# A decoder on one core: the clamp of the mixer's decay differences is computed on ScalarE instead of VectorE

## What is computed

```
dt = clip(softplus(dt + dt_bias), 0, 100)
A_cum = cumsum(dt * A)                                  # over the 128 tokens, falling, since A < 0
L = exp(where(l >= s, A_cum[l] - A_cum[s], -inf))       # the decays
Y = einsum('bzlhn,bzshn,bhzls,bzshp->bzlhp', C, B, L, hs * dt) + hs * D
out = rmsnorm_per_group(Y * silu(gate)) * norm_w @ out_proj_w.T
```

## Time and profile before

| | |
|---|---|
| time, median of 3 runs | 2916.17 us (2915.06 to 2918.78) |
| the profiled execution, its span from the first to the last instruction | 2919.1 us |
| PE busy | 2603.7 us (89%) |
| DVE busy | 1872.9 us (64%) |
| ACT busy | 1371.7 us (47%) |
| POOL busy | 1129.4 us (39%) |
| mixer stage | 382 to 1836 us of the span, 1454 us |

### The profile page before, as it was taken

How to read it: one execution, slowest core, us unless ns; L and a number is a source line. 1 busy time by engine, 2 the same in 40 slices (tenths; PEclk the granted TensorE clock), 3 DMA queues, 4 the chain that set the end, 5 groups by cost and what they waited for, 6 DMA issues and landing times. The chain is left out here.

```text
span 2919.1 us, 43490 instructions
## 1 busy us (share of the span) xinstructions
PE 2603.7 (89%) x14432; PEld 2118.4 (73%) x14432; DVE 1872.9 (64%) x3011; ACT 1371.7 (47%) x2589; POOL 1129.4 (39%) x889
## 2 busy tenths in 40 slices
PE   6677489999999999999999998699999999999958
PEld 4335377777777777777777776588888888888846
DVE  4565468688696886968859687454644645546453
ACT  2221156465464664646646464344544544545431
POOL 0000047565575655756557465322122221221210
PEclk9888789999999999999999998799999999999989
DMA  2100033032130321303213030101000000010010
GB/s 77 63 0 1 15 113 126 30 130 80 61 120 30 130 80 55 126 30 126 84 55 126 29 130 22 54 26 30 14 24 26 18 25 22 22 29 18 11 50 30
DMA packets 61999, 163.47 MB, mean 56 GB/s; under 512 B 8304, under 2 KB 8944, under 8 KB 53424
## 3 DMA queue, kind: packets, MB, share of 16 engines
q1 hardware_dynamic: 59232, 157.16, 15.9%
q10 hardware_dynamic: 2640, 4.47, 0.5%
HBM read 158.98 MB, written 2.62 MB: 55 GB/s over the span
## 5 line engine op out<-in xcount | busy, mean ns | idle before, releaser
L157 PE MATMUL bank<-XH,d_w_hi 128*128 128x512 f32 x1160 | 472.5, 407 | 32.8 <-POOL d_w_lo L1097 17.9
L159 PE MATMUL bank<-XH,d_w_lo 128*128 128x512 f32 x1160 | 458.7, 395 | 0.0
L158 PE MATMUL bank<-XL,d_w_hi 128*128 128x512 f32 x1160 | 457.1, 394 | 0.0
L1097 POOL TENSOR_TENSOR d_w_lo<-d_w,d_w_hi 128x512 fp32r<-128x512 f32 x144 | 223.9, 1555 | 322.8 <-ACT d_w_hi L982 322.7
L1200 DVE SCALAR_TENSOR_TENSOR d_hs<-bank,d_conv,d_hs 128x508 f32<-128x508 f32 (+2 forms) x384 | 279.5, 740 | 43.5 <-ACT d_hs L1003 34.5
L157 PEld LDWEIGHTS bank<-XH,d_w_hi 128*128 128x128 f32 x1160 | 220.4, 190 | 91.0 <-issue 25.4
L1122 POOL TENSOR_TENSOR d_decay<-d_decay,d_acg 128x1024 f32<-128x1024 f32 x128 | 270.3, 2132 | 0.0
L159 PEld LDWEIGHTS bank<-XH,d_w_lo 128*128 128x128 f32 x1160 | 220.3, 190 | 49.7
L158 PEld LDWEIGHTS bank<-XL,d_w_hi 128*128 128x128 f32 x1160 | 220.9, 190 | 44.1
L1127 POOL TENSOR_TENSOR d_gated_lo<-d_gated,d_gated_hi 128x512 fp32r<-128x512 f32 x128 | 165.7, 1297 | 206.2 <-ACT d_gated_hi L1031 206.2
L1233 DVE TENSOR_TENSOR d_decay<-d_decay,d_cb 128x1024 f32<-128x1024 f32 x128 | 181.3, 1457 | 76.4 <-ACT d_decay L1023 76.4
(11 more groups left out here) (282 smaller groups left out, 6689.1 us busy)
## 6 DMA issues: line engine op xcount, KB each, us to landing
d_decay<-running_sums SPq DMA_DIRECT2D x64, 1024.0 KB, 4.8
d_w<-in_L_w_groups SPq DMA_DIRECT2D x144, 256.0 KB, 3.5
e_w<-in_L_w_heads SPq DMA_DIRECT2D x80, 256.0 KB, 2.6
d_wo<-in_L_wo_groups SPq DMA_DIRECT2D x64, 256.0 KB, 4.8
X<-in_x SPq DMA_DIRECT2D x8, 256.0 KB, 9.1
b_ctx<-in_ctx SPq DMA_DIRECT2D x8, 256.0 KB, 5.6
e_ctx<-in_ctx SPq DMA_DIRECT2D x8, 256.0 KB, 2.7
out<-X SPq DMA_DIRECT2D x8, 256.0 KB, 2.0
```

The costliest lines, as they stand in the source:

```text
L157: pe.matmul(out, wh, xh, start=first, stop=False)
L158: pe.matmul(out, wh, xl, start=False, stop=False)
L159: return pe.matmul(out, wl, xh, start=False, stop=last)
L1097: pool.tensor_tensor(WL[:, w, :, :], WR[:, w, :, :], WH[:, w, :, :].bitcast(F32), ALU.subtract).then_inc(q["w_split"], 1)
```

## The change

The clamp leaves DVE's program, at all its places. `exp` on ACT gets a first pass of two instructions, `relu(-x)`, which wait for `diff` and raise `clamped`; the exponentials then take `exp(-x)` of the result. Since min(x, 0) = -relu(-x), the values are the same.

```diff
                 def exp(g, j):
                     for h in range(2):
+                        act.wait_ge(q["diff"], START + 2 * (g * JT + j) + h + 1)
+                        r = R[:, j % 2, :, tokens(h)]
+                        act.activation(r, r, ACT.Relu, scale=-1.0).then_inc(q["clamped"], 1)
+                    for h in range(2):
                         act.wait_ge(q["clamped"], START + 2 * (g * JT + j) + h + 1)
                         r = R[:, j % 2, :, tokens(h)]
-                        act.activation(r, r, ACT.Exp).then_inc(q["exp"], 1)
+                        act.activation(r, r, ACT.Exp, scale=-1.0).then_inc(q["exp"], 1)
...
-                def clamp(g, j):
-
-                    for h in range(2):
-                        v.wait_ge(q["diff"], START + 2 * (g * JT + j) + h + 1)
-                        r = R[:, j % 2, :, tokens(h)]
-                        v.tensor_scalar(r, r, 0.0, None, ALU.min).then_inc(q["clamped"], 1)
-
...
                 def group(g, last_group=False):
                     for j in range(JT - 1):
                         conv(g, 4 + 2 * j)
-                        clamp(g, j + 1)
                         gated(g, j)
                         xdt(g, j + 1)
                         scores(g, j + 1)
...
                         conv(g + 1, 1)
                         conv(g + 1, 2)
-                        clamp(g + 1, 0)
...
                     conv(0, i)
-                clamp(0, 0)
```

## The result

The changed kernel takes **3000.61 us** (median of 4 runs, 2992.52 to 3004.41) against 2917.48 us before (median of 4 runs, 2915.06 to 2919.75): ratio 1.0284, 95% interval 1.0267 to 1.0302. It is slower by 83 us; 2990 was forecast, with 2958 to 3020 as the range. The profiled execution is the shortest of the four, 2992.52 us with a span of 2990.8; the others took 8 to 12 us more. The mixer's last exponentials start 73.8 us later than before; what follows them takes 2.1 us less.

What follows compares the result with a forecast made beforehand. The prediction took the chain that readies the decays, not ACT's fullness, as the bound. 56 us serial plus 20 for PE's clock took the profiled span from 2919.1 to 2995, the median to 2992, with POOL's reliefs 2990 (2958 to 3020).

Steps and rivals of the forecast that it cites:

- The new cycle, 14.90 us: Mixer step round the chain: 4.72 us exponentials to projection, 5.82 to the gate, then 1.91, 0.53 and 1.92 to the exponentials.
- step to pair 1: Each group's first step: next projection at 601.38 against 601.02, +0.4 us, and 0.4 more for the prologue.
- step to pair 2: No margin before its scan: +1.92 and about 0.2 for POOL's later scalings, 2.1 us (1.4 in group 1).
- step to pair 3: 14.99 us before, 14.90 after: 0, DVE's gain paying for ACT's loss.
- steps to pairs 4, 5, 6: 14.57 us before, 14.90 after: +0.33 each, 1.0 per group in groups 2 to 8; 2.7 in group 1.
- step to pair 7: +1.92 us, less up to 0.45 if POOL's scaling is no longer slowed: 1.7.
- change of group: Seven times, the square right behind the exponentials, no slack on the path: +1.92 us each.
- The clock, +20 us: PE's longer waits lower its clock some fourteen times at 1.7 us; 20 us taken, bounds 0 and 48.
- The relief of POOL: Without the clamp, POOL's scaling before pair 7 falls from 1.49 us towards 1.04, up to 0.45 us less.
- DVE as the bound: Rival: DVE bounds the step, so 27 or 28 steps fall to 14.0 us, 16 us; 2893 or 2900; 3 in 100.
- The rival in which the clock holds: The serial sum alone, without falls of PE's clock: 2972 us, or 2965 with POOL's relief; 24 in 100.
- The one with all falls at double price: Rival: the clock falls further, 56 + 48 us and the eighth group, 3020 us and above; 12 in 100.

Runs made afterwards that it cites:

- Experiment 3: The changed kernel with the relu pass between the gate's two halves (at the change of group, ahead of an evacuation): 2895.72 us, ratio 0.9936 to the kernel before.
- experiment 11: The changed kernel with a second relu pass behind the first, changing no value: 3138.53 us, ratio 1.0775 to the kernel before.
- experiment 4: The changed kernel with 12 additional 128x512 matmuls on PE ahead of the scans of pairs 2 and 7: 2976.44 us, ratio 1.0217 to the kernel before.
- Experiment 2: The changed kernel with the clamp also kept on DVE, so both passes run: 3029.14 us, ratio 1.0393 to the kernel before.
- experiment 1: The kernel before with neither clamp nor relu, exponentials scaled by 1e-30: 2896.73 us, ratio 0.9938 to the kernel before.
- experiment 5: The changed kernel with two more DVE instructions in each half of `gated`, reading only PSUM: 2989.93 us, ratio 1.0258 to the kernel before.
- experiment 6: The changed kernel with the relu between the gate's halves in the steps, but still right before the exponentials at the change of group: 2920.87 us, ratio 1.0016.

## Why the prediction was right

*What bounds: the chain, not the busy share.* Right. Experiment 3 runs the same ACT work off the chain and the 83 us are gone; experiment 11 shows that the length of the pass is on the chain in every step.

*The price of the pass, 1.92 us.* Right: from the gate to the exponentials 3.80 us were measured and 3.83 taken; 3.80 - 1.91 = 1.89 is the pass.

*The new cycle, 14.90 us.* Right: the spacings of exponentials in steps 4 to 6 are 14.92 and 14.93 us. The sum round the chain gives the step to within 0.03 us, though no engine's work fills it.

*The steps one by one*, in the second group. Steps to pairs 1 and 3 are measured between the projections behind two scans, those to pairs 2 and 7 from such a projection to the next exponentials (which leaves the slower scan to the clock's term), those to pairs 4 to 6 between exponentials, and the change of group by PE's wait:

| term | forecast | measured |
|---|---|---|
| step to pair 1 | +0.4 | 14.36 - 14.01 = +0.35 |
| step to pair 2 | +2.1 | 13.60 - 11.58 = +2.02 |
| step to pair 3 | 0 | 14.87 - 14.99 = -0.12 |
| steps to pairs 4, 5, 6 | +1.0 | 3 x 0.36 = +1.08 |
| step to pair 7 | +1.7 | 13.24 - 11.81 = +1.43 |
| change of group | +1.92 | 2.66 - 0.82 = +1.84 |

The sum is 6.6 us per group against 7.1 forecast. From one group's first exponentials to the next one's, the mean of groups 2 to 7 went from 183.26 to 192.42 us, 9.16 more; the 2.6 us that are left I count as the clock (experiment 4, with the falls of pairs 2 and 7 gone, has 190.15). Six groups give 39.6 us serial and 15.4 left; group 1 with the prologue 8.4 + 3.0 = 11.4 (forecast 8.6) and group 8 7.4 (forecast 5.2) hold both kinds. Together they are the 73.8 us by which the mixer's last exponentials come later. My estimate is that 53 to 58 of them are serial, where the sum had 56; that it comes so near is in part luck, since groups 2 to 7 stay 3 us below their forecast and groups 1 and 8 lie 5 above theirs.

*The clock, +20 us.* The mechanism was right, the count nearly. All 16 scans of pairs 2 and 7 fell, 4 of 7 changes of group did, as forecast; 27.3 us more of full speed were lost in the mixer, and what of it shows in the time is the 15.4 us and a part of groups 1 and 8, by the same estimate 16 to 21. Experiment 4 takes the falls of pairs 2 and 7 away and wins 20 to 24 us. The other executions of the changed kernel took 8 to 12 us more than the profiled one; with a mean granted clock of 0.944 to 0.946 against 0.949 they had lost a little more clock. That is where the 10.6 us come from by which the median lies above 2990: the forecast of the profiled span, 2995, was 4 us too high, but the forecast took the median 2.9 us below the profiled span, as in the kernel before, and it lies 9.8 us above it.

*The relief of POOL.* In the step to pair 7 it came as forecast: the second scaling, which `wo_hi` waits for, takes 1.05 us in the changed kernel instead of 1.49, and the term is 0.5 us below 1.92. ACT and POOL there:

```profile
702.33 0.63 ACT L987 ACTIVATE d_wo_hi<-d_wo 128x512 fp32r<-128x512 f32 x1 [2.41 <-POOL d_wo L1112]
```

```profile
701.25 1.05 POOL L1112 TENSOR_TENSOR d_wo<-d_wo,d_nw 128x512 f32<-128x512 f32 x1
```

*What failed: the worth of the clamp's departure.* The rivals' sums had 7 us for it on POOL, the scalings alone. Experiment 2 shows some 30: the clamp also holds up `w_lo`, 1.76 against 1.29 us, in the steps of a kernel whose chain runs through ACT. My 14.90 us for a step took a POOL that is never late, without a row for it; had the clamp stayed, the same sum would have been 0.45 us short. That it came out right there was luck. Had I written the clamp's effect on POOL as a term, it would have read 15.4 less 0.45. The prologue is not a second miss, though its exponentials come 3.0 us later. ACT's first weight copy in the mixer already starts 1.13 us later (381.06 against 379.93), which no pass of the mixer can cause; the pass adds 1.89, but PE's first scan comes only 1.19 us later (405.00 against 403.81), so PE feels nothing of it there, and 0.34 in the step to pair 1.

*The busy times.* ACT's grew by 116 us instead of 134, and DVE's fell by 138 instead of 145 to 155. The forecast added up durations, and busy time counts instructions that overlap once: by durations ACT has 133.9 us more and DVE 150.7 less (154.7 of clamps and 30.1 of the decays' multiplication gone, 34.1 more for `gated`'s).

*The rivals.* DVE as the bound was worth 15 to 18 us (experiment 1), close to the 16 that I gave it, and experiment 3 collects them; in the change as it is the cycle through ACT, 14.92 us, lies above the 14.0 that it needed. The rival in which the clock holds is excluded by the stretches at 0.57 and 0.66. The one with all falls at double price did not come: 20 to 24 us, not 48.

## What to carry to other kernels

Price an instruction by its place: write the cycle across the engines as a sum of spacings from timelines, and compare it with the fullest engine. A pass that stood behind the wait of a half idle engine cost its full length wherever the chain had no slack; put into that wait, it was free (3000.6 against 2895.7 us with the same work). Where TensorE stood still for more than 3 us here, the loss came twice, as a wait and as a lower clock behind it, and moving one unneeded instruction from ahead of the late one (the second copy, 2850.6 us) repairs both.

## What the runs showed of the hardware

- DVE and POOL held each other up here, and the one that started second took longer. Take the clamp and the two multiplications of DVE whose operands all lie in SBUF. In the changed kernel from 500 us on, `w_lo` took 1.26 to 1.32 us in all 75 places where none of them was running at its start, also in the 47 where one started later, and 1.68 to 2.00 us in the 50 where one was. The scaling took 1.03 to 1.05 us in 21 places of the first kind and 1.48 to 1.51 in 35 of the second. `gated`'s multiplication of two SBUF tiles took 0.69 us when it started with POOL idle, and 0.75 to 1.83 when POOL's instruction had started first. Instructions of DVE that read PSUM left `w_lo` and the scaling at 1.31 and 1.06 (experiment 5), and `conv`'s taps, which read PSUM, took 0.73 to 0.75 us beside POOL or not. I had not expected this to reach ACT and PE with 30 us.
- The clock fell behind all 15 waits of 3.4 to 3.9 us ahead of a scan, behind 4 of 7 waits of 2.6 to 2.7 us at the changes of group (7 of 7 in experiment 6, with waits of the same length), and in the kernel before behind 5 of the 15 of 1.8 to 2.0 us. A fall costs about 1.7 us of full speed; a few cost twice that, such as this one of the changed kernel:

```profile
820.00:828.00 8.00, 5.72 (x38) 5.00 (x39) 6.86 (x9) 6.39 (x9) 5.48 (x3) 0.57 0.05 18
```

  Why one wait of the same length lowers it and another does not stays open.
- Additional matmuls whose result nobody reads made the changed kernel 20 to 24 us faster (experiment 4).
